# Rotary angles per half, V's first stores on SyncE's queue, a new order on ScalarE, and the convolution kernel's inputs loaded in attention

## The reference, cut to what matters

```python
q, k, v = x@Wq.T, x@Wk.T, x@Wv.T              # x: 32 batches x 32 tokens x 512; 32 q heads, 8 k/v heads of 128
q, k = rope(rmsnorm(q)*wq, pos), rope(rmsnorm(k)*wk, pos)   # pos = cache_seqlens[b] + t
k_all = concat(k_cache[block_table], k); v_all = concat(v_cache[block_table], v)   # 512 + 32 keys
o = softmax(mask(q@k_all.T * SCALE)) @ v_all @ Wo.T
K = s4_kernel(Lambda, p, q, Vc@Bp, Ct, step)  # 512 taps, by a transform; no dependence on x
x = x + causal_conv(o, K) + D*o
x = x + ffn(lora_linear(x))                   # linear with LoRA per batch, then linear + 8 gated rank-16 parts
```

## Time and profile before

| | us |
|---|---|
| runs (3): lowest, median, highest | 1266.29, 1268.01, 1268.69 |
| the profiled execution | 1267.51 |
| its span in the trace | 1265.5 |
| busy: TensorE, VectorE, ScalarE, GpSimd | 1232.9, 804.2, 789.2, 749.0 |
| granted TensorE clock, mean | 0.995 |

### The profile page before, as it was taken

One profiled execution on the slowest core, in us unless ns is written; L12 is line 12 of the kernel. 1 busy time (PEld: TensorE's weight loads), 2 busy tenths in 40 slices (PEclk: granted clock), 3 DMA queues, 4 the chain that ended last, 5 costly groups with the idle time before them and its releaser, 6 DMA issues.

```text
span 1265.5 us, 28738 instructions
## 1 busy us (share of the span) xinstructions
PE 1232.9 (97%) x7378; PEld 1036.5 (82%) x7378; DVE 804.2 (64%) x1725; ACT 789.2 (62%) x2258; POOL 749.0 (59%) x884
## 2 busy tenths in 40 slices
PE   7899999999999999999998999999999999999998
PEld 6678889999999987866776888898999999888756
DVE  5976667667766776952329766676676677655422
ACT  5676677777777774432336666777787777744320
POOL 4344468888888874433233444588888888754330
PEclk9999999999999999999999999999999999999999
DMA  6343289999999955306144342889989999534300
GB/s 236 117 134 124 96 231 231 225 234 232 236 237 235 232 146 183 143 1 200 50 145 125 118 136 101 226 225 233 232 231 238 234 233 237 133 111 152 90 31 34
DMA packets 147979, 214.82 MB, mean 170 GB/s; under 512 B 24950, under 2 KB 119480, under 8 KB 142137
## 3 DMA queue, kind: packets, MB, share of 16 engines
q1 hardware_dynamic: 130568, 204.86, 59.7%
q10 hardware_dynamic: 17328, 9.04, 2.5%
HBM read 203.33 MB, written 10.49 MB: 169 GB/s over the span
## 4 chain that ended last, share of the span: by engine, by line
PE 84%; SPq 5%; DVE 3%; issue 3%; ACT 3%; DMA 1%; ACTq 1%; DVEq 0%
PE PS L1130 16%; PE PS L1098 8%; PE PS L1197 5%; PE PS L992 5%; PE PS L990 5%; PE PS L996 5%; PE PS L1188 5%; PE PS L1194 5%; PE PS L1140 4%; PE PS L976 2%; PE PS L1239 2%; PE PS L1063 2%; SPq L464 2%; PE PS L1065 2%; PE PS L1081 2%
## 5 line engine op out<-in xcount | busy, mean ns | idle before, releaser
L624 POOL TENSOR_TENSOR kv_parts<-kv,k_hi 128x544 fp32r<-128x544 f32 x192 | 258.0, 1344 | 55.0 <-ACT k_hi L806 54.9
L1130 PE MATMUL PS<-probT,kv 128*128 128x128 f32 x2048 | 271.9, 276 | 0.0
L584 POOL TENSOR_TENSOR ring_parts<-ring,kv_parts 128x512 fp32r<-128x512 f32 x96 | 126.2, 1320 | 217.4 <-ACT kv_parts L687 189.2
L1130 PEld LDWEIGHTS PS<-probT,kv 128*128 128x128 f32 x2048 | 250.5, 193 | 0.0
L847 ACT ACTIVATE ring<-ring,smin 128x544 f32<-128x544 f32 x192 | 143.0, 745 | 93.2 <-DVE smin L1618 92.8
L1624 DVE COPY probT<-PS 128x512 f32<-128x512 f32 x256 | 175.5, 685 | 5.4 <-PE PS L1098 5.4
L1618 DVE CUSTOM_DVE_ANT_0 ring<-PS,mask,rq 128x544 f32<-128x544 f32 x192 | 149.8, 780 | 41.5 <-PE PS L1086 31.9
L646 POOL TENSOR_TENSOR ring_parts<-ring,kv_parts 128x512 fp32r<-128x512 f32 x64 | 84.1, 1317 | 100.6 <-ACT kv_parts L897 100.6
L612 POOL TENSOR_SCALAR ring<-ring,rinv 128x512 f32<-128x512 f32 x192 | 133.0, 693 | 0.0
L806 ACT ACTIVATE k_hi<-kv 128x544 fp32r<-128x544 f32 x192 | 124.5, 650 | 8.5 <-DMA kv<-k_new 2.8
L1098 PE MATMUL PS<-consts,ring 128*128 128x128 f32 x768 | 116.6, 275 | 2.1 <-DVE probT L1624 1.7
(11 more groups left out here) (219 smaller groups left out, 2790.4 us busy)
## 6 DMA issues: line engine op xcount, KB each, us to landing
kv<-in_kpages SPq DMA_DIRECT2D x512, 128.0 KB, 2.6
kv<-in_vpages SPq DMA_DIRECT2D x512, 128.0 KB
ring<-in_w SPq DMA_DIRECT2D x44, 1024.0 KB, 5.0
v_new<-kv ACTq DMA_DIRECT2D x16, 256.0 KB, 4.6
k_new<-kv ACTq DMA_DIRECT2D x16, 256.0 KB, 2.4
kv<-k_new SPq DMA_DIRECT2D x32, 128.0 KB, 2.6
kv<-v_new SPq DMA_DIRECT2D x32, 128.0 KB
kv<-in_xT SPq DMA_DIRECT2D x8, 256.0 KB, 5.1
```

What stands on the lines that cost most here:

```text
L624: nc.gpsimd.tensor_tensor(kbuf_lo(par)[:, :, g, :], kbuf(par)[:, :, g, :], k_hi[:, e % 2, :].rearrange("p (j t) -> p j t", t=PSIZE), ALU.s ...
L1130: mm = nc.tensor.matmul(PS[:, at:at + D], vbuf(bpar)[:, c, gg * D:(gg + 1) * D], probT[:, g % 2, c * P:(c + 1) * P], start=(c == 0 and a = ...
```

## The change

- `angles` works on 256 columns, this half's, instead of 512, at the beginning of each half and no longer once ahead of the loop. It begins with a wait for the end of the previous half (`out_ready`). The links between its operations are waits on a semaphore of its own. `trig` has half the size, and `pos` a tile of its own.
- ScalarE takes the two sines of 256 columns in both halves, as soon as `upper(1, c)` is done, ahead of V's stores. Its order after that is new; the diff shows it.
- V's first four tiles are stored by SyncE's queue, in the order 2, 3, 0, 1, ahead of the load of block 4. ScalarE issues only the stores of V's second half.
- The five inputs of the convolution kernel are loaded behind the last batch's pages and ahead of block 15, into 17920 to 18816 of `kv`, which attention does not use. The other scratch of the convolution kernel moves down.

```diff
@@ SBUF
-        svec = scratch(640)...  vcT = scratch(P)...  bpB = scratch(P)...  bp = scratch(4)...
+        svec = kv[:, 17920:18560]...  vcT = kv[0:NSTATE, 18560:18688]
+        bpB = kv[0:NSTATE, 18688:18816]  bp = kv[0:NSTATE, 18816:18817]
@@ SyncE
             with sp.Fori(0, HALVES) as h:
+                for k, m in enumerate((2, 3, 0, 1)):
+                    sp.wait_ge(v_read, h * (2 * TILES) + k + 1)
+                    sp.dma_start(vn_d[...], v_stage(0, m)...).then_inc(vn_out[m % 2], 16)
                 with sp.Fori(0, 2) as i:
                     for n in range(4, 8):
                         load_w(h, n, i)
...
+                with sp.If(h < 1):
+                    for dst, src in [(vcT, vcT_d), (bp, bp_d), ...]:
+                        sp.dma_start(dst, src).then_inc(space_in, 16)
                 load_w(h, 15)
                 sp.wait_ge(new_turned, QUADS * (h + 1))
                 load_w(h, 14)
                 sp.wait_ge(o_done, QUADS * (h + 1))
-                with sp.If(h < 1):
-                    for dst, src in [(vcT, vcT_d), (bp, bp_d), ...]:
-                        sp.dma_start(dst, src).then_inc(space_in, 16)
@@ ScalarE
-                for m in range(2, TILES): store_v(0, m)
-                for c in range(2): upper(2, c)
-                with act.If(h < 1):
-                    act.wait_ge(ang_ready, 1)
-                    nc.scalar.activation(trig[:, 0:512], angs, ACT.Sin).then_inc(trig_ready, 1)
-                    nc.scalar.activation(trig[:, 512:1024], angc, ACT.Sin).then_inc(trig_ready, 1)
-                for c in range(2, KC): upper(2, c)
-                for n in range(KU):
-                    ...
+                act.wait_ge(ang_ready, h + 1)
+                nc.scalar.activation(trig[:, 0:NANG], angs, ACT.Sin).then_inc(trig_ready, 1)
+                nc.scalar.activation(trig[:, NANG:2 * NANG], angc, ACT.Sin).then_inc(trig_ready, 1)
+                store_v(0, 2); store_v(0, 3)
+                squares(0); upper(2, 0); upper(2, 1)
+                squares(1); upper(2, 2); upper(2, 3)
+                squares(2); store_v(0, 0); store_v(0, 1)
+                squares(3); root(0, rstd[:, 1, :], rstd[:, 0, :])
+                for n in range(TILES, KU):
+                    upper(3, n % TILES); squares(n)
+                    if n >= LAG: store_k(n - LAG)
+                root(1, rstd[:, 1, :], rstd[:, 0, :])
@@ TensorE, block 1
-                            if m == 2: pe.wait_ge(ang_ready, 1)
-                            elif m == 3: pe.wait_ge(trig_ready, 2)
+                            if m == 2: pe.wait_ge(ang_ready, h + 1)
+                            elif m == 3: pe.wait_ge(trig_ready, 2 * h + 2)
@@ VectorE
-            angles()
             with dve.Fori(0, HALVES) as h:
-                dve.wait_ge(trig_ready, 2)
+                angles(h)
+                dve.wait_ge(trig_ready, 2 * h + 2)
```

More of the change, by code:

```diff
@@ L258, in scratch @@
             return kv[:, free[0] - n:free[0]]
[L260 to L263, removed]
+        svec = kv[:, 17920:18560].rearrange("p (v n) -> p v n", n=NSTATE)
+        vcT = kv[0:NSTATE, 18560:18688]
+        bpB = kv[0:NSTATE, 18688:18816]
+        bp = kv[0:NSTATE, 18816:18817]
         vv_ = scratch(512)
@@ L280, in build @@
         krow = big2_[0:1, :]
[L282 to L286, removed]
+        NANG = TILES * D // 2
+        ang = bank(2)[:, 0:NANG]
+        angn = part(12800, NANG)
+        angs = part(13312, NANG)
+        angc = bank(3)[:, 0:NANG]
         misc_in = sem("misc_in")
@@ L702, in store_v @@
                         .then_inc(v_read, 1)
-                    order = m if col else (m + 2) % TILES
-                    act.wait_ge(v_read, h * (2 * TILES) + col * TILES + order + 1)
-                    act.dma_start(vn_d[ds(h * HB + 4 * m, 4), :, col * D:(col + 1) * D]
+                    if col == 0:
+                        return
+                    act.wait_ge(v_read, h * (2 * TILES) + TILES + m + 1)
+                    act.dma_start(vn_d[ds(h * HB + 4 * m, 4), :, D:2 * D]
                                   .rearrange("b (t a) d -> (b t) a d", a=GU),
-                                  v_stage(col, m).rearrange("p (a d) -> p a d", a=GU))\
+                                  v_stage(1, m).rearrange("p (a d) -> p a d", a=GU))\
                         .then_inc(vn_out[m % 2], 16)
@@ L763, in _ @@
                     nc.scalar.activation(gain[:, 0:1], dls[:, 1:2], ACT.Exp, scale=-1.0).then_inc(gain_ready, 1)
[L764 to L767, removed]
-                with act.If(h < 1):
-                    act.wait_ge(ang_ready, 1)
-                    nc.scalar.activation(trig[:, 0:512], angs, ACT.Sin).then_inc(trig_ready, 1)
-                    nc.scalar.activation(trig[:, 512:1024], angc, ACT.Sin).then_inc(trig_ready, 1)
-                for c in range(2, KC):
-                    upper(2, c)
-                for n in range(KU):
-                    if n >= TILES:
-                        upper(3, n % TILES)
+                act.wait_ge(ang_ready, h + 1)
+                nc.scalar.activation(trig[:, 0:NANG], angs, ACT.Sin).then_inc(trig_ready, 1)
+                nc.scalar.activation(trig[:, NANG:2 * NANG], angc, ACT.Sin).then_inc(trig_ready, 1)
+                store_v(0, 2)
+                store_v(0, 3)
+                squares(0)
+                upper(2, 0)
+                upper(2, 1)
+                squares(1)
+                upper(2, 2)
+                upper(2, 3)
+                squares(2)
+                store_v(0, 0)
+                store_v(0, 1)
+                squares(3)
+                root(0, rstd[:, 1, :], rstd[:, 0, :])
+                for n in range(TILES, KU):
+                    upper(3, n % TILES)
                     squares(n)
-                    if n < 2:
-                        store_v(0, n)
                     if n >= LAG:
                         store_k(n - LAG)
-                    if n % TILES == TILES - 1:
-                        root(n // TILES, rstd[:, 1, :], rstd[:, 0, :])
+                root(1, rstd[:, 1, :], rstd[:, 0, :])
                 act.wait_ge(half_free, h + 1)
@@ L1342, in positions @@
                 dve.wait_ge(misc_in, 16 * NMISC)
-                link(V.tensor_copy(pos, lens_i[:, :]))
+                link(V.tensor_copy(pos[:, :], lens_i[:, :]))
                 link(V.tensor_copy(lens_b[:, :], lens_bi[:, :]))
```

64 lines of the change are left out of this document (39 added, 25 removed).

## The result

The changed kernel takes **1257.3 us** (median of 4 runs, 1256.73 to 1258.46), against 1268.1 for the kernel before in runs on the same chip: a ratio of 0.9913, 95% interval 0.99 to 0.9927, 10.8 us faster. The profiled execution took 1256.7, its span 1254.8. The forecast was 1255.2; 2.0 us of its 12.8 are missing.

What follows compares the result with a forecast made beforehand. The prediction took TensorE, 84% of the chain of waits, to bound the kernel. Its terms 4.5 + 5.4 + 2.9 = 12.8 us took the median 1268.0 to 1255.2, chance 0.70, with a range of 1252.0 to 1261.0.

Steps and rivals of the forecast that it cites:

- Wo's third head: Half 0: earlier convolution inputs remove TensorE's 2.77 us wait and the low clock after it; 4.5 us, bounds 0 and 4.8.
- Beginning of half 0: Projections: K's fourth unit (unit 3) starts at 32.5 instead of 37.90; 5.4 us, bounds 3.9 and 5.6.
- Beginning of half 1: Projections: unit 3 could start at 665.5 instead of 668.48; 2.9 us, bounds 1 and 3.1.
- The rule on table sets: ScalarE: a set change costs 1.28 us by the trace; the skill's 2.66 would make the sum 11.1 instead of 12.8.
- Attention as long as before in both halves: Sign of being right: attention does not lengthen in either half when the projections end earlier.
- rival 1: Attention: the stream of pages sets the pace and the projections' gain is given back, leaving 4.5 us, 1263.5; chance 0.07.
- Rival 4: Block 4's weights come late behind V's stores on SyncE's queue; both halves 9 us late, 5.2 slower, 1273; chance 0.04.

Runs made afterwards that it cites:

- before_spv: The kernel before with one part alone: V's first stores issued by SyncE; angles, ScalarE's order and the convolution's loads stay. 1267.28 us.
- before_order: The kernel before with ScalarE's new order alone; angles for both halves, V's stores by ScalarE and the convolution's loads stay. 1266.06 us.
- after_pair: The changed kernel with V's cached pages of batches 2 and 3 in 8 two-page transfers instead of 16, at fixed pages. 1254.10 us (0.9886).
- after_oldang: The changed kernel with the old full-width angles, once ahead of the loop, and full-width sines in half 0 only. It lost 0.3 to 0.5 us.
- before_conv: The kernel before with only the convolution's inputs loaded at the end of attention. 1264.12 us (0.9966).
- before_lessv: The kernel before with a quarter of the columns of V's cached pages loaded for batches 2 and 3 of each half. 1269.41 us beside 1268.5.
- after_actv: The changed kernel with V's first stores issued by ScalarE again, four in each half. 0.9 us slower than the changed kernel.
- after_peel: The changed kernel with the loads of batches 2 and 3 written out ahead of SyncE's loop, but whole, as a control. 1256.89 us (0.9903).
- after_more: The changed kernel with batches 2 and 3's loads written out, plus 8 issues of 64 bytes ahead of batch 2's pages in half 0. 1257.42 us.

## Why the prediction was right, and what was off

**Wo's third head.** Forecast 4.5, measured 4.55. `steps` follows head 1's remainder, no later head waits, the clock stays at 1.00.

**Beginning of half 0.** Forecast 5.4, measured 5.1: unit 3 at 32.77, forecast 32.5. The angles took 4.8 us (5.1 forecast). The set that I had loaded back ahead of V's copies, 1.28 us, is not in the trace: no load stands between the sines and `root`'s at 32.75. That slack was not needed, for the squares of tile 3 wait for TensorE, and unit 3 waits for them. Turn 0 was forecast at 39.9 and came at 39.48; block 4's first rounding at 50.5 and came at 50.77.

**Beginning of half 1.** Forecast 2.9, measured 2.7. The reason I gave, V's stores off ScalarE together with squares as they fall due, fits: before_spv has 2.41 with the stores alone, before_order 1.45 with the order alone, each in one execution. For half 0 the same reason was put too strongly ("this is what lets the squares be taken as they come"): with new order and new angles, ScalarE's own stores would have cost 0.6 us of the 5.1.

**The rule on table sets.** The forecast took 1.28 us for a change of set and set the Trainium skill's 2.66 (ScalarE: Activation LUTs, "What ACT_TABLE_LOAD costs") against it. The load at 18.84 is followed by the first sine at 20.13, 1.29 us later, in a chain that by the page would have had another 1.38 in it; in half 1 the load lies in idle time. The trace shows 1.28 and has no place for the rest.

**Attention: the term that failed.** "Attention as long as before in both halves", a term of zero, with rival 1 against it at 0.07. In half 0 it was 1.6 us longer (311.6 from the last projection's matmul to Wo's first instead of 309.9; in half 1 311.1 in both), and by the ledger it gave back 2.3 us after having kept the clock. So rival 1 was right in its mechanism, for 1.6 of the 8.3 us that it priced. It named the stream of pages, by its DMA share of 0.97; the trace and two runs put SyncE's queue beside the bytes, full with 34 issues for each batch, and do not part the two. My argument against the rival was that TensorE was never idle there and that the first pages move with the projections. Both were true of the kernel before and said nothing of its reserve, which was small: before_order, 2.15 us ahead as attention began, already lost that and more. In half 1 attention began at -10.73 and ended at -10.7 to -11.3, as forecast, but by luck: it won 1.2 us of clock that the forecast did not have and lost 0.6 to 1.2 of it again. ScalarE waited 4.4 us for keys there from 780 to 1110 us, 1.6 in the kernel before, and in after_pair, where it waited 0.5, half 1 won 2.2 us.

**The sum.** 4.55 + 5.09 + 2.70 = 12.3, less 1.6 in attention, is 10.7; forecast 12.8. Rival 4 did not come: block 4 went out at 32.47 and was there at 50.77.

## What to carry to other kernels

Before a gain ahead of a streamed stage is counted in full, ask what reserve the queue that feeds the stage has: add up the issues of one round on that queue (here 18.6 us) and set the sum beside the round (19.2); in this kernel so full a queue gave back part of what came earlier, though hardly an engine waited for it before. Parts of a change that take work off the same engine ahead of the same deadline do not add up: in half 0 two of them brought 1 us each alone and 4.6 together, and the third then brought 0.5. And look at the granted clock of a control before you use it as one: here one stretch of 3.4 us at the lower level hid what was to be measured.

## What the runs showed of the hardware that was not expected

An issue of a DMA has a price in the queue even with almost nothing to carry: 8 of 64 bytes took 2.3 us, 0.29 each. 16 of 128 KB took 7.3 for V's pages (0.46 each) and 8 of 256 KB took 5.1 (0.64 each); the first and the last had fixed addresses, so size and addressing are not told apart.

A table set was loaded again behind the sines only where these stood in a conditional block: in the kernel before, in after_oldang (23.36, 1.28 us) and in before_order (23.68), and in half 1 of before at 657.52, where no sine ran at all. With the sines outside of it, V's copies and the squares follow at once. No run tried the block alone.

The kernel before spreads more: 10 runs taken together went from 1266.5 to 1270.7 us at a granted clock of 0.993 to 0.997, beside 5 of the changed kernel from 1256.2 to 1257.9 at 0.999 to 1.000. The changed kernel's first four reached 1258.5, two of them at 0.997. The stretches at the lower level behind turn 0 and behind the third head are gone from every trace in which the waits there are gone. The other way round it does not hold: before_spv waited 3.7 us at the third head and its clock stayed at 1.00 there, and the wait of some 2.5 us at half 1's turn had such a stretch behind it in before_conv (671.3) and before_lessv (677.7) but not in the kernel before. The stretches at the beginnings of attention come and go from kernel to kernel (after_actv, after_peel and after_more have both, the first and the last with no longer waits ahead of them than the changed kernel), and what decides there stays open.
